# Counting the two halves of a group's outputs apart in the expert stage of a one-core Trainium2 kernel

## The reference, cut to what matters

```
tidx, tw = _route(xf, router_w, correction_bias)      # 8 of 64 experts for each token, and their weights
h   = relu(x @ up_w[e]) ** 2                          # 256 -> 128, for each token of expert e
y   = h @ down_w[e]                                   # 128 -> 256
out = x + shared(x) + sum over the 8 choices of tw * y
```

## Time and profile before

| | us |
|---|---|
| median of 3 runs | 1869.3 (1865.94 to 1871.79) |
| the profiled execution | 1868.09 |
| its span | 1866.2 |
| last stage, first scatter to last | 1385.2 to 1837 |

### The profile page before, as it was taken

The page is one execution under the profiler, slowest core; times in us unless marked ns, Lnnn a source line. Parts: engine busy times, 40 slices in busy tenths (PEclk is TensorE's granted clock), DMA queues, the critical chain, the costliest instruction groups (busy, mean ns, idle before and its releaser), DMA issues. The chain is left out here.

```text
span 1866.2 us, 35427 instructions
## 1 busy us (share of the span) xinstructions
PE 1542.3 (83%) x12186; PEld 1216.8 (65%) x12187; DVE 1187.6 (64%) x2849; ACT 826.3 (44%) x1614; POOL 940.9 (50%) x840
## 2 busy tenths in 40 slices
PE   5699999987888869999999999975058888888880
PEld 2588888864655547776777776654058877776770
DVE  2677677745777655578878778787024455666674
ACT  2233333323545334565565555643036564555550
POOL 1233333335665521115555555567627767776672
PEclk9899999989999989999999999997579999999995
DMA  5278458011000000001111111136666678998875
GB/s 152 61 192 219 117 152 235 1 32 51 25 13 24 12 24 1 1 2 52 61 58 55 61 61 58 55 117 244 181 210 189 191 221 265 285 278 259 268 210 158
DMA packets 151371, 226.33 MB, mean 121 GB/s; under 512 B 24779, under 2 KB 123730, under 8 KB 149079
## 3 DMA queue, kind: packets, MB, share of 16 engines
q1 hardware_dynamic: 109062, 115.11, 22.1%
q0 software_dynamic: 27648, 67.44, 10.2%
q10 hardware_dynamic: 14544, 42.21, 7.0%
HBM read 110.31 MB, written 122.75 MB: 125 GB/s over the span
## 5 line engine op out<-in xcount | busy, mean ns | idle before, releaser
L1927 POOL DMA_INDIRECT y_rows<-se_ys,se_yidx x320 | 325.2, 1016 | 162.8 <-issue 95.8
L1100 POOL DMA_INDIRECT x_slots<-wide,a_sidx x256 | 257.2, 1005 | 72.5 <-issue 72.5
L443 POOL TENSOR_TENSOR e_hl<-e_h,e_hh 128x512 fp32r<-128x512 f32 x80 | 103.5, 1294 | 227.7 <-ACT e_hh L427 227.7
L1089 POOL TENSOR_TENSOR flat<-flat,a_rs 128x512 f32<-128x512 f32 x64 | 69.8, 1091 | 269.7 <-DVE a_rs L1581 269.7
L1970 PE MATMUL ps<-wide,se_hT 128*128 x640 | 157.8, 390 | 31.2 <-DVE se_ys L2060 30.9
L1947 PE MATMUL ps<-ident,se_xs 128*128 128x128 f32 x640 | 89.1, 285 | 100.8 <-DMA se_xs<-x_slots 83.2
L1958 PE MATMUL ps<-se_xsT,se_up 128*128 128x128 f32 x1280 | 166.1, 285 | 5.3 <-DVE se_hT L2049 4.3
L1958 PEld LDWEIGHTS ps<-se_xsT,se_up 128*128 128x128 f32 x1280 | 155.8, 199 | 13.6 <-issue 9.9
L1947 PEld LDWEIGHTS ps<-ident,se_xs 128*128 128x128 f32 x640 | 74.9, 146 | 121.4 <-issue 84.6
L1970 PEld LDWEIGHTS ps<-wide,se_hT 128*128 128x128 f32 x640 | 117.2, 193 | 50.6 <-issue 37.5
L1991 ACT COPY se_up<-w_up 128x256 f32 x320 | 105.8, 402 | 99.5 <-issue 78.6
(11 more groups left out here) (283 smaller groups left out, 3613.8 us busy)
## 6 DMA issues: line engine op xcount, KB each, us to landing
x_slots<-wide SPq DMA_DIRECT2D x40, 1032.0 KB, 14.3
se_xs<-x_slots SPq DMA_DIRECT2D x80, 516.0 KB
se_got<-y_rows ACTq DMA_DIRECT2D x64, 512.0 KB, 4.8
w_up<-in_up SPq DMA_DIRECT2D x8, 1024.0 KB, 18.1
y_rows<-se_ys,se_yidx POOLq DMA_INDIRECT x320
wide<-in_xT SPq DMA_DIRECT2D x2, 2048.0 KB, 10.2
flat<-in_x SPq DMA_DIRECT2D x8, 512.0 KB, 3.9
x_slots<-wide,a_sidx POOLq DMA_INDIRECT x256, 2.9
```

The lines of the kernel that those rows point to most:

```text
L1100: pool.indirect_dma_start(out=x_slots, out_offset=bass.IndirectOffsetOnAxis(ap=sidx[:, r % 2, t, k_:k_ + 1], axis=0), in_=stage[:, t, k_, ...
L1927: pool.indirect_dma_start(out=y_rows, out_offset=bass.IndirectOffsetOnAxis(ap=yidx[:, w % 2, b:b + 1], axis=0), in_=ys[:, w % 2, b, :], in ...
```

## The change

`y_ps` becomes two counts, `ya_ps` (blocks 0 and 1) and `yb_ps` (blocks 2 and 3); each `y_out` becomes two, for the scatters of the two halves. PE issues the four matmuls of blocks 0 and 1 when ACT has read PSUM for the group before, then the four of blocks 2 and 3 when DVE has. ACT waits only for `ya_ps` and the first half's scatters of group g - 2, DVE only for `yb_ps` and the second half's. POOL waits for `y_act` and issues two scatters, then waits for `y_dve` and issues two. The indices of group n are made in turn n, after DVE's `ys` of group n - 2, in a ring of four; POOL waits for `h_ready` of the group, which comes later on DVE than the indices. ACT's relu, which overwrites `hT`, waits for `yb_ps`.

```diff
-                yidx = sb("yidx", [P, 2, GB], I32)
+                yidx = sb("yidx", [P, TR, GB], I32)
@@ POOL
-                            pool.wait_ge(y_act, g + 1)
-                            pool.wait_ge(y_dve, g + 1)
-                            pool.nop(nofuse=True)
-                            for b in range(GB):
-                                pool.indirect_dma_start(
-                                    out=y_rows, out_offset=bass.IndirectOffsetOnAxis(ap=yidx[:, w % 2, b:b + 1], axis=0),
-                                    in_=ys[:, w % 2, b, :], in_offset=None,
-                                    bounds_check=T * K2 - 1, oob_is_err=False).then_inc(y_out[w % 2], 16)
+                            pool.wait_ge(h_ready, g + 1)
+                            for side, done in enumerate((y_act, y_dve)):
+                                pool.wait_ge(done, g + 1)
+                                pool.nop(nofuse=True)
+                                for b in range(2 * side, 2 * side + 2):
+                                    pool.indirect_dma_start(
+                                        out=y_rows,
+                                        out_offset=bass.IndirectOffsetOnAxis(ap=yidx[:, (w - 2) % TR, b:b + 1], axis=0),
+                                        in_=ys[:, w % 2, b, :], in_offset=None,
+                                        bounds_check=T * K2 - 1, oob_is_err=False).then_inc(y_out[w % 2][side], 16)
@@ PE
-                            wait(pe, y_act, g)
-                            wait(pe, y_dve, g)
-                            for b in range(GB):
...
-                            last.then_inc(y_ps, 1)
+                            for side, (free_, full) in enumerate(((y_act, ya_ps), (y_dve, yb_ps))):
+                                wait(pe, free_, g)
+                                for b in range(2 * side, 2 * side + 2):
...
+                                last.then_inc(full, 1)
@@ ACT
-                            wait(act, y_ps, g - 1)
+                            wait(act, yb_ps, g - 1)
...
-                            act.wait_ge(y_ps, g + 1)
-                            wait(act, y_out[w % 2], half(q, w, 2) * 16 * GB)
+                            act.wait_ge(ya_ps, g + 1)
+                            wait(act, y_out[w % 2][0], half(q, w, 2) * 32)
...
-                                for sent in y_out:
-                                    act.wait_ge(sent, done * 16 * GB)
+                                for sent in y_out[0] + y_out[1]:
+                                    act.wait_ge(sent, done * 32)
@@ DVE
-                            dve.wait_ge(y_ps, g + 1)
-                            wait(dve, y_out[w % 2], half(q, w, 2) * 16 * GB)
-
-                            dve.tensor_scalar(yidx[:, w % 2, :], tail[:, (w - 2) % TR, :, 0], -1.0, float(T * K2),
-                                              ALU.mult, ALU.add)
+                            dve.wait_ge(yb_ps, g + 1)
+                            wait(dve, y_out[w % 2][1], half(q, w, 2) * 32)
+                            dve.nop(nofuse=True)
...
+                        if live(0):
+                            dve.wait_ge(t_dve, n + 1)
+                            wait(dve, y_out[w % 2][0], half(q, w, 2) * 32)
+                            dve.nop(nofuse=True)
+                            dve.tensor_scalar(yidx[:, w, :], tail[:, w, :, 0], -1.0, float(T * K2), ALU.mult, ALU.add)
```

More of the change, by code:

```diff
@@ L1871, in slot_experts @@
                 summed, added, stored = sem("summed"), sem("added"), sem("stored")
-                y_out = [sem("y_out0"), sem("y_out1")]
-                t_ps, t_act, t_dve, up_ready, z_ps, r_ready, h_ready, y_ps, y_act, y_dve = (
+                y_out = [[sem("y_out0a"), sem("y_out0b")], [sem("y_out1a"), sem("y_out1b")]]
+                t_ps, t_act, t_dve, up_ready, z_ps, r_ready, h_ready, ya_ps, yb_ps, y_act, y_dve = (
                     sem(n) for n in ("t_ps", "t_act", "t_dve", "up_ready", "z_ps", "r_ready", "h_ready",
-                                     "y_ps", "y_act", "y_dve"))
+                                     "ya_ps", "yb_ps", "y_act", "y_dve"))
                 block = ph.enter_context(nc.Block())
@@ L1922, in turn @@
                             g = n - 2
-                            pool.wait_ge(y_act, g + 1)
-                            pool.wait_ge(y_dve, g + 1)
-                            pool.nop(nofuse=True)
-                            for b in range(GB):
-                                pool.indirect_dma_start(
-                                    out=y_rows, out_offset=bass.IndirectOffsetOnAxis(ap=yidx[:, w % 2, b:b + 1], axis=0),
-                                    in_=ys[:, w % 2, b, :], in_offset=None,
-                                    bounds_check=T * K2 - 1, oob_is_err=False).then_inc(y_out[w % 2], 16)
+                            pool.wait_ge(h_ready, g + 1)
[8 more added lines that the diff above has]
+                                        bounds_check=T * K2 - 1, oob_is_err=False).then_inc(y_out[w % 2][side], 16)
                     pipeline(pool, turn)
                     for w in range(2):
-                        pool.wait_ge(y_out[w], NG // 2 * 16 * GB)
+                        for side in range(2):
+                            pool.wait_ge(y_out[w][side], NG // 2 * 32)
                 @block.tensor
@@ L1966, in turn @@
                                 pe.wait_ge(wd_in, (-(-EARLY // WCOLS) - (EARLY - E2) // WCOLS) * 16)
-                            wait(pe, y_act, g)
-                            wait(pe, y_dve, g)
-                            for b in range(GB):
[L1970 to L1973, removed]
-                            last.then_inc(y_ps, 1)
+                            for side, (free_, full) in enumerate(((y_act, ya_ps), (y_dve, yb_ps))):
+                                wait(pe, free_, g)
+                                for b in range(2 * side, 2 * side + 2):
+                                    last = pe.matmul(ps[:, 4 + side, (b % 2) * D:(b % 2 + 1) * D],
+                                                     hT[:, w % 2, b, :],
+                                                     w_dn[:, bass.ds(e[b], 1), :].rearrange("p o n -> p (o n)"),
+                                                     start=True, stop=True)
+                                last.then_inc(full, 1)
                     pipeline(pe, turn)
```

## The result

The changed kernel takes 1860.5 us (median of 18 runs) against 1868.5 for the kernel before, run in turn on the same chips: a ratio of 0.9959 with a 95% interval of 0.9946 to 0.9972. It is **8.0 us faster**, where 16.4 were forecast. The profiled execution has a span of 1858.5 us against 1866.2.

What follows compares the result with a forecast made beforehand. POOL's scatters were taken to bound the last stage, from 1385 us on, with stalls after turn 28. Gains of 14.3 + 4.4 + 1.0 less 3.3 made 16.4 us, so 1869.3 became 1853 us; range 1845 to 1869.

Steps and rivals of the forecast that it cites:

- the scatter ring: POOL after turn 28: two groups take 11.4 to 11.8 us against POOL's 10.3; separate counts remove 14.3 of 17.6 us stall.
- two long waits of POOL: POOL's two idle times of some 4.3 us, 112 scatters apart, no releaser among the engines; left in, no gain counted.
- What comes back: Denser DMA traffic from faster POOL makes landings and `xs` loads longer: 3.3 us lost, bounds 0 and 18 us.
- the two gaps left in: POOL's gaps at 1752.62 and 1759.89: 3.3 us of stall kept because a 7.68 us `xs` load held PE.
- Long first scatters: First scatters of a group after turn 28, 1.16 us after a stall against 0.99 without: 4.4 us gained.
- Products in halves: The first scatter of the stage waits for half the products and no indices: 1.0 us gained, once.
- The second wait point on POOL and the indices: POOL's added mid-group wait taken at nothing, bounds 0 and 22 us; index making at the end of DVE's turn hidden.
- the slower rival: POOL's second wait point costs up to 0.28 us in each of 80 groups, more than the stalls: 1878 us, 12%.
- the port rule: Two-port VectorE operations keep GpSimd from writing descriptors; 0.17 us for each of 80 index makings would give back 14 us.
- The transfers take over: Scatter landings grow from 5.7 to 7.9 us after turn 28, so about 8 us are won: 1862 us, 22%.

## Why the prediction was wrong, by its own steps

**The bound, and the scatter ring: right.** The stalls ended by DVE's `ys` went as soon as the two halves were counted apart. With the next bound out of the way the whole of them went: with four `xs` buffers the change takes first scatter to last from 446.7 us to 419.7. Of these 27 us, 17.4 are the stall ahead of first scatters (the prediction saw 17.6 and counted on 14.3), 7.4 the two long waits of POOL, which it left in, and some 2 the shorter busy time (4.4 forecast). So its 19.7 us before anything was given back had the ring about right.

**"What comes back": the step that failed.** It had 3.3 us, taken over from the two gaps left in behind the longest load. I had looked at PE's waits for `xs` in the kernel before, 8.7 us in five, and at 1.2 us less of cover. But this is a ring, as the scatters are, and should have been worked out like theirs. With the load of 7.68, 0.2 until the transposes, 1.0 of transposes and 0.9 of copies it takes 9.8 us for two groups, against POOL's 10.3. With the median load of the kernel before, 5.5, it takes 7.6, so at the old load times there was room. What the prediction priced far too low is that loads would be longer and that a ring of two has no place for it: 8.2 us is all it can bear, less when PE is at its lower clock. The runs show what stood in its place: 9 of 41 loads over 8.2 us, and 20.3 us of stall ahead of first scatters where there had been 20.6. The ring of loads gave back all that the ring of scatters had cost; four buffers for `xs` bring it to nothing.

**The two long waits of POOL: wrong, and the measured gain is mostly theirs.** I left 8.6 us of them in as a fixed cost, because the number of scatters is the same. In the changed kernel the first is gone and the second is 2.18 us (1.33 and 1.55 in its second trace), with four buffers 1.43. In the stage 9.9 us were won, 6.7 of them here and 3.8 by shorter scatters; the first scatter starts 2.5 us later in that trace, and the rest of the kernel is 0.3 shorter, which makes the 7.7 of the span. So it is in good part luck that the time lies in the range: the term with 14.3 of the 16.4 us gave nothing, and one priced at nothing gave 6.7. The waits are not part of the ring's stall: in the kernel before with half of `got` that stall is gone and they are still 3.90 and 3.51 us. Nor do the moved indices (5.00 and 4.66 with them alone) or the halved products (still one of 1.71 with joined products) account for them. What is left is that the scatters are counted apart and that POOL waits in mid-group. What they wait for the profile doesn't say (`issue`), and it wasn't tried.

**Long first scatters: right in kind.** Busy time over 0.985 a scatter fell from 10 us to 6; 4.4 were forecast.

**Products in halves: mis-sized.** I priced them once, at the start of the stage, at 1.0 us. There the gain can't be seen: the first scatter starts between 1383.5 and 1389.8 in these traces, with the change or without. Over all groups they are likely worth some 7 us once POOL is the bound (not shown, as said above).

**The second wait point on POOL and the indices: right at nothing.** Ahead of third scatters the stall is 1.0 us over all 80 groups in the changed kernel and nothing with four buffers, so the slower rival is dead. Moving the indices alone did nothing either (0.9994). The scatters in 1400:1500 took 0.98 or 0.99 us after the change, so by this trace the port rule that I weighed from the Trainium skill ("SBUF — State Buffer", "SBUF: two separate sides") gave back nothing here.

**The rivals.** "The transfers take over" had the time (1862) and the resource, but not the mechanism, and its time is luck: 38 groups at 0.3 us are 11.4 us and not the 8 it says, so its terms give 1858. It had scatters landing later in their own ring, after 7.9 us, and the DMA engines near their end at 0.91; in fact a half's last scatter lands after a median of 5.1 us in 1540:1780, the loads came late in another ring, with the engines less busy than before, and at 303 GB/s they still weren't the bound. The 361 GB/s that was set beside the limit of about 358 from the Trainium skill ("DMA: Bandwidth & Descriptors", Specifications) is from a window of 2 us; another in the kernel before, 1542:1544, reads 392 at a share of 1.05, so windows this short do not test that limit. The 8 us fall in the range given, 1845 to 1869; what was wrong is the forecast inside it.

## What to carry to other kernels

When a change loosens one ring of buffers, work out every other ring on the same stage in the same way: the latency of the transfer, plus the work that frees the buffer, per turn of the ring, against the pace that you expect afterwards. The waits of the old trace don't give that, and its usual load doesn't either: here the circle had 2.7 us of room at the median load, PE waited five times from 1400 us on, and then the loads grew by 1.2 us in the median and by up to 2.3 at the long end. Compare the longest transfers with what the ring can bear. And try both remedies together: four load buffers alone were worth nothing, the split counts alone 4 to 8 us, the two 27.

## What the runs showed of the hardware

POOL's two idle times of 4.64 and 4.54 us after scatter 113 and scatter 225 shrank to nothing and 2.18 us when the two halves of a group were counted apart, although the scatters were the same in number and size; taking the ring's stall away by less traffic left them at 3.90 and 3.51. With 256 of some 1540 KB a group left out (half of `got`; 251 GB/s for 282 in 1560:1700), the median load of 516 KB took 4.2 us for 5.5 in the kernel before. After a wait of 5.26 us PE did a turn of 32 matmuls in 7.2 us that otherwise takes 4.4, with a granted clock of 0.62 in that window, so a late load cost more than its lateness. On one chip every kernel tried ran 8 to 9% longer (the kernel before 2017 us for 1867), with other waits; a ratio from there doesn't test a theory made on the others.
